# The order of VectorE's and GpSimd's work at the opening of the last batch of a two-layer graph attention kernel

## The reference

```python
h = relu(layernorm(x))
x = x + L0(h, adj)      # f = h W^T; one head
h = relu(layernorm(x))
x = x + L1(h, adj)      # f = h W^T + b; four heads
# in each layer and head:
logits = leaky_relu(s_src[i] + s_dst[j], 0.2); logits = where(adj[i, j], logits, -big)
out[i] = sum_j softmax_j(logits)[i, j] * f[j]
```

## Time and profile before

| | before |
|---|---|
| median of 3 runs | 2777.57 us (2777.02 to 2782.05) |
| the profiled execution: its own time | 2781.38 us |
| the profiled execution: span, first to last instruction | 2779.2 us |
| mean granted TensorE clock, share of full | 0.953 |
| busy: TensorE / weight loads / VectorE / ScalarE / GpSimd | 89% / 80% / 72% / 59% / 50% |
| matmuls of layer 1 (L846, L852), 7680 each | 966.1 and 755.6 us |
| VectorE's bits (L1105, L1109) | 335.0 and 395.7 us |
| VectorE's own compares in phase B and in two groups of AB (L1085), 320 | 183.5 us |

### The profile page before, as it was taken

How to read it: one execution, slowest core, us unless ns; L and a number is a source line. 1 busy time by engine, 2 the same in 40 slices (tenths; PEclk the granted TensorE clock), 3 DMA queues, 4 the chain that set the end, 5 groups by cost and what they waited for, 6 DMA issues and landing times. The chain is left out here.

```text
span 2779.2 us, 56693 instructions
## 1 busy us (share of the span) xinstructions
PE 2467.9 (89%) x22166; PEld 2233.7 (80%) x22166; DVE 2011.5 (72%) x3326; ACT 1626.1 (59%) x3058; POOL 1385.4 (50%) x1757
## 2 busy tenths in 40 slices
PE   4996999979998799979999699996999979995786
PEld 3774999869997699968998599985999769994786
DVE  1557777587776777776777777768777677776996
ACT  4015666566665656657566566656666566562664
POOL 2113455545554455553555445563555535554576
PEclk9998999989999899998999899998999989997898
DMA  7641244313432144322443224431444213200010
GB/s 131 76 61 28 36 79 74 47 32 66 72 56 51 27 68 71 51 51 35 66 68 48 54 32 74 81 53 28 61 74 61 43 36 58 50 17 24 24 39 16
DMA packets 197737, 147.26 MB, mean 53 GB/s; under 512 B 143072, under 2 KB 144224, under 8 KB 197472
## 3 DMA queue, kind: packets, MB, share of 16 engines
q1 hardware_dynamic: 179040, 110.07, 16.8%
q0 software_dynamic: 18432, 33.56, 14.7%
HBM read 193.60 MB, written 50.66 MB: 88 GB/s over the span
## 5 line engine op out<-in xcount | busy, mean ns | idle before, releaser
L655 ACT ACTIVATE shared<-Rb,w 128x512 int8<-128x512 f32 x1728 | 1079.1, 718 | 309.2 <-DVE shared L1105 309.2
L827 PE MATMUL accA<-S,shared 128*128 128x257 f32 x4096 | 970.5, 390 | 61.0 <-DVE shared L1033 57.4
L846 PE MATMUL accB<-Sw,shared 128*128 128x195 bf16 x7680 | 966.1, 248 | 10.8 <-DVE shared L1109 8.8
L827 PEld LDWEIGHTS accA<-S,shared 128*128 128x128 f32 x4096 | 769.2, 193 | 165.9 <-DVE shared L1033 65.6
L852 PE MATMUL accB<-Sv,shared 128*128 128x130 f16 x7680 | 755.6, 221 | 0.0
L1033 DVE SCALAR_TENSOR_TENSOR shared<-Rb,w,mask 128x512 f32<-128x512 f32 x512 | 422.2, 839 | 387.5 <-PE accA L827 341.8
L846 PEld LDWEIGHTS accB<-Sw,shared 128*128 128x128 fp8e4 x7680 | 635.9, 98 | 53.4 <-issue 12.9
L852 PEld LDWEIGHTS accB<-Sv,shared 128*128 128x128 fp8e4 x7680 | 570.4, 98 | 0.0
L474 POOL TENSOR_SCALAR shared<-shared 128x260 f32<-128x260 f32 x128 | 144.2, 1127 | 635.5 <-ACT shared L697 630.7
L1105 DVE TENSOR_TENSOR shared<-shared,mask 128x512 uint32<-128x512 uint32 x432 | 335.0, 776 | 138.0 <-ACT shared L655 98.5
L1109 DVE TENSOR_TENSOR shared<-shared,mask 128x512 uint32<-128x512 uint32 x512 | 395.7, 773 | 10.4
(11 more groups left out here) (103 smaller groups left out, 2381.1 us busy)
## 6 DMA issues: line engine op xcount, KB each, us to landing
Rb<-R_dram SPq DMA_DIRECT2D x160, 256.0 KB, 3.4
adj_bytes<-in_adj POOLq DMA_DIRECT2D x128, 256.0 KB, 5.3
xb<-in_x SPq DMA_DIRECT2D x32, 512.0 KB, 3.9
out<-xb SPq DMA_DIRECT2D x32, 512.0 KB, 2.8
mask<-adj_bytes SPq DMA_TRANSPOSE x128, 4.4
shared<-in_W SPq DMA_DIRECT2D x2, 256.0 KB, 3.0
R_dram<-R_rows SPq DMA_DIRECT2D x8, 32.0 KB, 1.8
a_cols<-in_a SPq DMA_DIRECT2D x8, 0.2 KB, 11.0
```

Of the source, the lines that this page charges most:

```text
L655: last = nc.scalar.activation(cmp[:, slot, jj // 2, of_pair(jj % 2, 0, CI)], Rb[:, h, :], ACT.Sign, bias=w[1][:, JG * g + jj, h:h + 1], sc ...
L827: last = nc.tensor.matmul(accA[:, k, 0:F + 1], tiles[:, j % RING, k * P:(k + 1) * P], S0[:, j, 0:F + 1], start=j == 0, stop=j == NJ - 1)
L846: nc.tensor.matmul(acc[:, bank, col:col + NS], bits[:, g % BRING, 1, jj // 2, of_pair(jj % 2, k * P, P)], Sw[:, j, h, :, :].rearrange("p a ...
```

## The change

In phase B the parts of quarters 2 to 4 leave `features` and enter the first chunk's steps: VectorE's order becomes parts 1, `mean(1)`, high 1, then group 0 (compare, n bits, s bits), parts and high 2, group 1, parts and high 3, parts and high 4, group 2, group 3, and so on as before. GpSimd's order in phase B becomes product 1, rest 1, product 2, rest 2, product 3, rest 3, product 4, rest 4. ScalarE's, TensorE's and SyncE's orders stay. Phases A and AB stay; `split_features` and `high` become functions of VectorE's block, with the phase as an argument, unchanged in what they do.

```diff
     def vector_order(kind, events):
-        work = [e for e in events if e[0] in ("A", "G", "X1", "X2", "X3")]
+        work = [e for e in events if e[0] in ("A", "G", "X1", "X2", "X3", "PART")]
...
-            elif e[0] in ("X1", "X2", "X3"):
+            elif e[0] in ("X1", "X2", "X3", "PART"):
                 out_order += [e]
...
     STEP_B = order(0, 1, 0)
+
+    STEP_B_FIRST = [STEP_B[0], ("PART", 1), STEP_B[1], ("PART", 2), ("PART", 3)] + STEP_B[2:]
...
             for c in range(NC):
-                steps("B", STEP_B, B, c)
+                steps("B", STEP_B if c else STEP_B_FIRST, B, c)
...
                     pool.tensor_tensor(raw_of(t), raw_of(t), vs.to_broadcast([P, CH * H, CF]), ALU.mult)\
                         .then_inc(S["n_made"], 1)
-                    if t:
+                    if kind == "B":
+                        rest(t)
+                    elif t:
                         rest(t - 1)
-                rest(NC - 1)
+                if kind != "B":
+                    rest(NC - 1)
...
-                    split_features(0)
+                    split_features(ph, 0)
                     mean(1)
-                    for t in range(1, NC - 1):
-                        split_features(t)
-                        high(t - 1)
-                    split_features(NC - 1, [0])
-                    high(NC - 2)
-                    if not both:
-                        split_features(NC - 1, [1])
-                        high(NC - 1)
+                    if both:
+                        for t in range(1, NC - 1):
+                            split_features(ph, t)
+                            high(ph, t - 1)
+                        split_features(ph, NC - 1, [0])
+                        high(ph, NC - 2)
+                    else:
+                        high(ph, 0)
...
                 for e in vector_order(kind, events):
+                    if e[0] == "PART":
+                        split_features(ph, e[1])
+                        high(ph, e[1])
+                        continue
```

More of the change, by code:

```diff
@@ L891, in mean_variance, with split_features, high @@
                 last.then_inc(S[f"mv_ready{L}"], 1)
+            def split_features(ph, t, halves=(0, 1)):
+                js = slice(CH * t, CH * t + CH)
+                i = NC * (ph - 1) + t
+                raw = S1[:, js, :].rearrange("p j (h e) -> p (j h) e", h=H)[:, :, 0:CF]
+                parts = Sw[:, js, :, :, :].rearrange("p j h a e -> p (j h) a e")
+                if 0 in halves:
+                    if t == 0:
+                        dve.wait_ge(S["ones_ready"], ph)
+                        dve.wait_ge(S["exp_ready"], 4 * ph)
+                        dve.wait_ge(S["x2_ready"], H * NC * (ph - 1) + 1)
+                    else:
+                        dve.wait_ge(S["sw_ready"], i)
+                    ws = wv[:, js, :].rearrange("p j h -> p (j h)").unsqueeze(2)
+                    nc.vector.tensor_tensor(split, raw, ws.to_broadcast([P, CH * H, CF]), ALU.mult)\
+                        .then_inc(S["s_made"], 1)
+                    dve.wait_ge(S["s_made"], i + 1)
+                    nc.vector.tensor_copy(parts[:, :, 0, :], split).then_inc(S["s_chain"], 1)
+                    dve.wait_ge(S["s_chain"], 3 * i + 1)
+                    nc.vector.tensor_tensor(split, split, parts[:, :, 0, :], ALU.subtract)\
+                        .then_inc(S["s_chain"], 1)
+                if 1 in halves:
+                    dve.wait_ge(S["s_chain"], 3 * i + 2)
+                    nc.vector.tensor_copy(parts[:, :, 1, :], split).then_inc(S["s_chain"], 1)
+                    dve.wait_ge(S["s_chain"], 3 * i + 3)
+                    nc.vector.tensor_tensor(parts[:, :, 2, :], split, parts[:, :, 1, :], ALU.subtract)\
+                        .then_inc(S["sw_ready"], 1)
+            def high(ph, t):
+                dve.wait_ge(S["n_made"], NC * (ph - 1) + (t + 1))
+                nc.vector.tensor_copy(Sv[:, CH * t:CH * t + CH, :, 0, :].rearrange("p j h e -> p (j h) e"),
+                                      S1[:, CH * t:CH * t + CH, :]
+                                      .rearrange("p j (h e) -> p (j h) e", h=H)[:, :, 0:CF])\
+                    .then_inc(S["n_high"], 1)
             def features(kind, ph):
@@ L944, in mean @@
                             .then_inc(S["misc_used"], 1)
[L946 to L980, removed]
                 both = kind == "AB"
@@ L1014, in features @@
                     if both:
-                        split_features(NC - 1, [1])
-                        high(NC - 1)
+                        split_features(ph, NC - 1, [1])
+                        high(ph, NC - 1)
                     wait_alone(dve, S["misc_used"], misc_before_layer(kind, ph, 0) + 3)
```

## The result

The changed kernel took 2790.74 us (median of 5 runs, 2783.84 to 2796.45), the kernel before 2779.22 us beside it (5 runs, 2777.02 to 2782.05). The ratio is 1.0038, 95% interval 1.0020 to 1.0055: **slower, by 5.6 to 15.3 us**, which is little but clear of the scatter. The forecast was 8.8 us.

A forecast was written before the change was run, and what follows sets the result against it. It took the last batch's opening, up to TensorE's end of head 0, to set a relay without slack; front wait, uncovered compares and lower clock delay that end by 8.8 us: 2777.57 + 8.8 = 2786.4, range 2782.5 to 2791.5.

The forecast's parts named there:

- Step 1: VectorE's first compare in the last batch waits 6.4 us for the Rb load, three quarters of parts queued behind it.
- Step 2: Group 0's compare, mask and xor on VectorE take 3.18 us undisturbed, with GpSimd idle by then.
- Step 3: Quarter 2's parts on VectorE take 7.39 us, keeping the 2.85 us subtract beside GpSimd's product.
- Step 4: Group 1's bits on VectorE take 5.09 us; the mask also needs that quarter's low part.
- Step 5: Quarter 3 takes 7.39 us and quarter 4 8.64 to its high part, which starts 11.1 us later.
- Step 6: ScalarE's compares of groups 2 and 3 lose their cover; group 3's bits are ready 10.1 us later.
- Step 7: TensorE starts group 2 at the lower clock after idling; groups 2 and 3 end head 0 8.8 us later.
- Step 8: All four moves and three more chunks shift by 8.8 us; ScalarE's compare barely stays covered, else up to 0.9 more.
- rival (a): TensorE is at the higher clock when group 2 comes: +6.7 us, 2784.2; chance 0.13.
- Rival (b): Lower clock for all eight sets (+1.8) or VectorE's lag at the second move (+0.9): 2787.3 to 2789.1; chance 0.17.
- Rival (c): GpSimd's passes no longer stall VectorE, 6.66 us of stalls vanish: delay 2.2 us, 2779.7; chance 0.06.
- rival (d): The Rb wait costs nothing because the load lands ahead of it: +2.4 us left, 2780; chance 0.02.

The follow-up runs named there:

- e1: Changed kernel, but quarter 2's parts ahead of group 0's compare and quarter 3's ahead of group 1's; 2781.88 us (kernel before 2776.44 beside it).
- e7: Changed kernel, but the last batch's four first Rb loads issued in reverse head order, head 0's last; 2787.13 us (kernel before 2775.68 beside it).
- a2: The changed kernel itself measured again with more runs (11, and 15 of before); 2784.88 us against 2778.03, ratio 1.0027.
- e9: Changed kernel plus 224 extra matmuls on TensorE between groups 1 and 2 of the first head; 2787.23 us (kernel before 2777.80 beside it).
- e11: e9 with VectorE's four additions of the mean moved into its idle time ahead of group 2's mask; 2782.43 us (kernel before 2778.03 beside it).
- e2: Changed kernel, but ScalarE compares groups 2 and 3 behind quarter 2's low part, not quarter 4's; 2780.44 us (kernel before 2776.44 beside it).
- e8: Changed kernel plus 175 extra matmuls on TensorE between groups 1 and 2 of the first head; 2785.62 us (kernel before 2775.68 beside it).

## Why the prediction was right, step by step

The direction and the size held: +8.8 us forecast; 8.88 and 7.91 by the stretch of two executions, 5.0 to 10.0 in the larger comparison. The time itself, 2786.4, lies between the two medians. The first, 2790.74, is near the top of the range, but no cost that the range had allowed for was found: the stretch was 8.88 longer. The rest is put down to scatter, of its five runs and of the kernel before, whose median beside it is 1.65 above the one the forecast built on.

Step 1 said 6.4 us of waiting; 6.33, and e1 and e7 show that it is paid. The load landed 4.1 us after its issue again, as the row had it, and not 2.6. (The Trainium skill gives the fit that step 1 set beside the row for transfers that GpSimd issues; SyncE issues this one.) Step 2, 3.18; 3.19 (2547.76 to 2550.95). Step 3, 7.39; 7.39, with the 2.85 us stall kept. Step 4, 5.09; 5.20, the mask waiting 0.27 us for the low part, the guard that step 4 named. Step 5, 7.39 and 8.64; 7.40 and 8.63. The last high part was to come 11.1 later: 11.21. Step 6, 10.1 later for the bits: 10.23, with 6.08 us of idle from the high part to ScalarE's first finished group. Step 7, 8.8 later for head 0's end: 9.15, the two groups taking 6.89 where 6.8 was put.

**Step 8 held in one of the two executions.** It said that the moves shift with head 0's end, and that ScalarE's compare ahead of the second move keeps its cover, "barely". In a2 it did: the second move waits 0.89 us for GpSimd and is 9.25 us later than before, as the first is (9.31). In the first execution it did not: the second move stands directly behind the compare that VectorE released, and is 8.47 us later where the first is 9.15. Two things used up the 2.05 us by which the compare had been ahead. VectorE had fallen further behind than head 0's end: the bits by 1.1 us (10.23 against 9.15), the compare by 1.5 (10.63). And GpSimd's ten steps for head 0, which step 8 took as fixed, needed 8.96 us instead of 9.75; that is where 0.8 us of head 0's delay went. Their first and last in before, and in the changed kernel:

```profile
2593.90 0.95 POOL L474 TENSOR_SCALAR shared<-shared 128x260 f32<-128x260 f32 x1 [16.05 <-ACT shared L697]
...
2602.96 0.69 POOL L495 TENSOR_TENSOR xb<-xb,shared 128x256 f32<-128x256 f32 x1 [0.18 <-POOL shared L491]
```
```profile
2596.67 0.88 POOL L479 TENSOR_SCALAR shared<-shared 128x260 f32<-128x260 f32 x1 [14.05 <-ACT shared L702]
...
2604.71 0.92 POOL L500 TENSOR_TENSOR xb<-xb,shared 128x256 f32<-128x256 f32 x1 [0.18 <-POOL shared L496]
```

The two chains run level there, and which of them ends last changes from one execution to the next. e9 to e11 show the consequence: head 0's end alone sets the rest only when it is later; the 2 us that TensorE's clock takes off the first move come back at the next.

This makes rival (a) wrong in its price. With TensorE at the higher clock it gave 2784.2, 2.1 us less; e9 made that case and the stretch lost 0.77, no more than two executions of one kernel differ by (0.97). Rival (b), the lag coming through at the second move, happened in the first execution without the extra time I had put on it, since the lag took the place of head 0's delay instead of adding to it. Rival (c) fell with the rows of the changed kernel, rival (d) with the 6.33 us row.

**What was luck.** That 8.88 is within a tenth of 8.8. The shift is not handed on unchanged, as step 8 has it: the four moves of chunk 0 are 9.15, 8.47, 9.51 and 9.50 us later than in before, the end 8.88; in a2 9.31, 9.25, 9.42, 8.84 and 7.91. From the last move of one chunk to that of the next it is 47.33 and 47.24 us in before, 46.72 and 47.31 in the changed kernel, 46.75 and 46.73 in a2. With one trace of before and two of the changed kernel the size is known to about a microsecond.

What stays open: why executions of one kernel differ in this way. The traces show where: GpSimd's ten steps do not take the same time each time. For the third head of chunk 0 they took 9.26 us in before and in the first execution of the changed kernel and 8.67 in a2, for the second head 9.34, 10.40 and 9.51. No run here was made to find out what they depend on.

## What to carry to other kernels

Before a consumer is interleaved with the work that feeds it, look at what else its first instruction waits for: on an engine that works in order, a load that was hidden becomes a stall for everything queued behind it, here 6.3 us for three quarters of parts that had nothing to do with it. Look likewise at what the moved work had been covering on another engine, because that cover goes with it. And a relay that is late in one hand-over may have a second chain level with it: repairing one of them shows next to nothing in the end until the other is moved too, as e9 and e11 show.

## What the runs showed of the hardware

A bit instruction on 32-bit words with two inputs in on-chip memory took 2.54 us instead of 0.69 beside a GpSimd pass over 1040 elements (e2), as the casts, subtracts and compares do; I had counted stalls for the parts and the compares alone. TensorE, busy for 15.39 us up to 2585.97 in e8, had a granted clock of 1.00 (2.4 GHz) in the window to 2588, 0.83 in the next microsecond and 0.50 (1.2 GHz) from 2589, and began its real work there at the lower level: the pause of 4.45 us gave back all that had been bought.
